# Two of five one-hot tiles per step move from VectorE to ScalarE in the last part of a graph kernel's scatter

## The reference

```python
q = (x_norm @ Wq + bq).reshape(num_nodes, NH, HD)
k = (x_norm @ Wk + bk).reshape(num_nodes, NH, HD)
v = (x_norm @ Wv + bv).reshape(num_nodes, NH, HD)
scores = jnp.einsum('ehd,ehd->eh', q[src], k[tgt]) / np.sqrt(HD).astype(np.float32)
scores = scores + (curv @ Wc + bc)
smax = jax.ops.segment_max(scores, tgt, num_segments=num_nodes)
p = jnp.exp(scores - smax[tgt])
probs = p / jax.ops.segment_sum(p, tgt, num_segments=num_nodes)[tgt]
messages = (probs[:, :, None] * v[tgt]).reshape(scores.shape[0], -1)
out = jnp.zeros_like(x).at[src].add(messages)
```

## Time and profile before

| | us |
|---|---|
| median of 3 runs | 8923.19 |
| lowest to highest | 8923.06 to 8924.19 |
| the profiled execution, its own time | 8924.33 |
| its span, first to last instruction | 8922.3 |

### The profile page before, as it was taken

One profiled execution on the slowest core, in us unless ns is written; L12 is line 12 of the kernel. 1 busy time (PEld: TensorE's weight loads), 2 busy tenths in 40 slices (PEclk: granted clock), 3 DMA queues, 4 the chain that ended last, 5 costly groups with the idle time before them and its releaser, 6 DMA issues. The chain is left out here.

```text
span 8922.3 us, 172430 instructions
## 1 busy us (share of the span) xinstructions
PE 6527.5 (73%) x29604; PEld 5175.7 (58%) x29605; DVE 5892.7 (66%) x18026; ACT 2572.9 (29%) x6876; POOL 6456.8 (72%) x6759
## 2 busy tenths in 40 slices
PE   6555555555788888888888988888745677666667
PEld 4433333333555555555688888888734566666555
DVE  4444444444566666666688888888854776766767
ACT  3111111111011111111355555555433333333322
POOL 6777777776777777777677777777757777777752
PEclk7566666666555555555555555555556777877778
DMA  5222222222222222222455555555435666666652
GB/s 199 61 65 67 66 65 66 66 65 64 54 63 62 62 63 62 62 63 62 102 137 136 136 136 136 136 136 136 121 81 126 154 154 152 156 154 154 154 139 77
DMA packets 1031683, 926.16 MB, mean 104 GB/s; under 512 B 210913, under 2 KB 911477, under 8 KB 1031495
## 3 DMA queue, kind: packets, MB, share of 16 engines
q0 software_dynamic: 214496, 443.25, 18.3%
q1 hardware_dynamic: 627671, 341.67, 15.1%
q10 hardware_dynamic: 189400, 139.98, 7.8%
HBM read 734.34 MB, written 192.49 MB: 104 GB/s over the span
## 5 line engine op out<-in xcount | busy, mean ns | idle before, releaser
L599 PE MATMUL stage_ps_agg<-stage_hot,stage_msg 128*128 128x128 f32 x6656 | 1587.4, 414 | 1221.6 <-DMA stage_msg<-xt,stage_index 890.7
L599 PEld LDWEIGHTS stage_ps_agg<-stage_hot,stage_msg 128*128 128x128 f32 x6656 | 1377.5, 306 | 1519.2 <-issue 662.4
L1174 POOL DMA_INDIRECT big<-q,stage_index x1664 | 1597.2, 960 | 547.3 <-issue 489.0
L1631 POOL DMA_INDIRECT slots<-big,stage_index x1664 | 1603.2, 963 | 510.6 <-issue 442.0
L588 POOL DMA_INDIRECT stage_msg<-xt_next,stage_index x1664 | 1570.7, 944 | 531.0 <-issue 520.3
L588 POOL DMA_INDIRECT stage_msg<-xt,stage_index x1664 | 1570.3, 944 | 530.3 <-issue 487.6
L631 DVE TENSOR_TENSOR big<-big,stage_ps_agg 128x128 f32 x3328 | 951.7, 286 | 1350.5 <-PE stage_ps_agg L599 989.8
L577 ACT ACTIVATE stage_index<-big 128x4 int32 (+1 forms) x832 | 170.3, 205 | 3607.3 <-PE stage_ps_agg L599 3509.1
L1668 PE MATMUL stage_ps_val<-nodes_a,big 128*128 x3328 | 672.4, 366 | 656.8 <-ACT big L1594 635.1
L1668 PEld LDWEIGHTS stage_ps_val<-nodes_a,big 128*128 128x128 f32 x3328 | 592.4, 267 | 719.0 <-issue 718.3
L1684 PE MATMUL stage_ps_sums<-stage_hot,big 128*128 128x128 f32 x4160 | 754.9, 345 | 112.0 <-DVE big L1804 107.1
(11 more groups left out here) (306 smaller groups left out, 9675.2 us busy)
## 6 DMA issues: line engine op xcount, KB each, us to landing
big<-slots SPq DMA_DIRECT2D x1976, 66.0 KB
big<-in_edge_attr_dram SPq DMA_DIRECT2D x1664, 64.0 KB
stage_trow<-targets ACTq DMA_DIRECT2D x830, 128.0 KB
stage_msg<-xt,stage_index POOLq DMA_INDIRECT x1664
stage_msg<-xt_next,stage_index POOLq DMA_INDIRECT x1664
big<-q,stage_index POOLq DMA_INDIRECT x1664
slots<-big,stage_index POOLq DMA_INDIRECT x1664
xt_next<-stage_xo SPq DMA_DIRECT2D x98, 256.0 KB, 2.9
```

The source lines that it names most:

```text
L599: last = self.nc.tensor.matmul(self.ps[h][:, j, :], self.msg[q][:, j, :], self.hot[h][:, j, :], start=True, stop=True)
L1174: pool.indirect_dma_start(qrow[q][:, j * D:(j + 1) * D], None, d["q"], bass.IndirectOffsetOnAxis(ap=index[q][:, j:j + 1], axis=0))\
L1631: pool.indirect_dma_start(d["slots"], bass.IndirectOffsetOnAxis(ap=index[q][:, j:j + 1], axis=0), total[q][:, j, :], None).then_inc(s_sc[q ...
```

## The change

In the last part VectorE's one-hot instruction covers three tiles (j = 2, 3, 4), 384 columns. ACT makes the other two (j = 0, 1): for each tile |place - n| into the new buffer `away` (two instructions of 128 columns, the place as a bias per partition), then relu(1 - away) for both tiles in one instruction of 256 columns into `hot`. For whole numbers this is 1 where n equals the place and 0 elsewhere.

ACT does it in the same queue in which it issues its two DMAs: a step waits for the freed buffer, issues the DMAs of step y, then makes the one-hot rows of step y-2. ACT's first four steps are written out, 12 turns of four steps follow in the loop, and the one-hot rows of the last two steps stand behind it. TensorE waits for one more semaphore (`s_act_hot`) in these steps. SP's part is the same as before, written in place of the shared function. The seven other parts don't change.

```diff
+    turns, SHARE, BY_SP, BY_ACT = GP // SLOTS, 3, 2, 2
+    away = slots("away", 2, [P, BY_ACT, P])
+    s_act_hot, s_away = m.sem("c_act_hot"), m.sem("c_away")
...
-        last_part(act, mybir.EngineType.Activation, SHARE, SET)
+        for q in range(SLOTS):
+            act.wait_ge(s_sc[q], TURNS * 16 * G + at[q])
+
+        def make_hot(y, h):
+            ring_index(act, s_place, y + 1, passed)
+            for j in range(BY_ACT):
+                nc.scalar.activation(away[h][:, j, :], t["iota"][:, :], ACT.Abs, scale=-1.0, bias=place[h][:, j:j + 1])\
+                    .then_inc(s_away, 1)
+            ring_index(act, s_away, (y - (PARTS - 1) * GP) * BY_ACT + BY_ACT, passed)
+            nc.scalar.activation(hot[h][:, 0:BY_ACT, :], away[h][:, :, :], ACT.Relu, bias=1.0, scale=-1.0)\
+                .then_inc(s_act_hot, 1)
+
+        def step(i, q):
+            y = i * SLOTS + (q + (PARTS - 1) * GP)
+            act.wait_ge(s_sum, y + 1)
+            r = offsets(nc, mybir.EngineType.Activation, pair_row, y * STRIDE + SHARE, SET - SHARE, (K - 1) * P)
+            for j in range(SHARE, SET):
+                act.dma_start(rows[q][:, j, :], d["slots"][bass.ds(r[j - SHARE], P), :]).then_inc(s_rows[q], 16)
+            if not isinstance(i, int) or y >= (PARTS - 1) * GP + 2:
+                make_hot(y - 2, q % 2)
+
+        for q in range(SLOTS):
+            step(0, q)
+        act.addr_align(256, max_nops=1)
+        with act.Fori(1, turns) as i:
+            for q in range(SLOTS):
+                step(i, q)
+        for y in range(SETS - 2, SETS):
+            make_hot(y, y % 2)
...
                 pe.wait_ge(s_hot, x.at() + (1 - FIRST))
+                if not x.within(0, FIRST, GROUPS + LAG):
+                    pe.wait_ge(s_act_hot, x.at() + (1 - LAG - GROUPS))
...
+                by_act = 0 if x.within(1, FIRST, GROUPS + LAG) else BY_ACT
...
-                nc.vector.tensor_tensor(hot[h][:, :, :], ps_lane[:, 0:P].unsqueeze(1).to_broadcast([P, SET, P]),
-                                        place[h][:, :].unsqueeze(2).to_broadcast([P, SET, P]), ALU.is_equal)\
+                nc.vector.tensor_tensor(hot[h][:, by_act:SET, :],
+                                        ps_lane[:, 0:P].unsqueeze(1).to_broadcast([P, SET - by_act, P]),
+                                        place[h][:, by_act:SET].unsqueeze(2).to_broadcast([P, SET - by_act, P]),
+                                        ALU.is_equal)\
                     .then_inc(s_hot, 1)
```

More of the change, by code:

```diff
@@ L1528, in scatter @@
     marks = (0, FIRST, GROUPS, LAST)
-    turns, SHARE, BY_SP = GP // SLOTS, 3, 2
+    turns, SHARE, BY_SP, BY_ACT = GP // SLOTS, 3, 2, 2
+    away = slots("away", 2, [P, BY_ACT, P])
+    s_act_hot, s_away = m.sem("c_act_hot"), m.sem("c_away")
     block = m.stack.enter_context(nc.Block())
[L1532 to L1543, removed]
     def load_targets(engine, g, q):
@@ L1575, in _ @@
                         sp.dma_start(rows[q][:, j, :], d["slots"][bass.ds(r[j], P), :]).then_inc(s_rows[q], 16)
-        last_part(sp, mybir.EngineType.SP, 0, SHARE)
+        for q in range(SLOTS):
+            sp.wait_ge(s_sc[q], TURNS * 16 * G + at[q])
+        sp.addr_align(256, max_nops=1)
+        with sp.Fori(0, turns) as i:
+            for q in range(SLOTS):
+                y = i * SLOTS + (q + (PARTS - 1) * GP)
+                sp.wait_ge(s_sum, y + 1)
+                r = offsets(nc, mybir.EngineType.SP, pair_row, y * STRIDE, SHARE, (K - 1) * P)
+                for j in range(SHARE):
+                    sp.dma_start(rows[q][:, j, :], d["slots"][bass.ds(r[j], P), :]).then_inc(s_rows[q], 16)
     @block.scalar
```

## The result

| | before | after |
|---|---|---|
| median of 22 runs each, us | 8924.40 | 8937.99 |
| lowest to highest | 8920.56 to 8927.70 | 8935.70 to 8943.86 |
| span of the profiled execution | 8922.3 | 8934.1 |

The change makes the kernel slower by 13.6 us: the ratio is 1.0016, with a 95% interval of 1.0010 to 1.0022. The forecast was 8935, 12 us more than before, in a range of 8922 to 8944.

A forecast was written before the change was run, and what follows sets the result against it. The prediction took SP's DMA-issuing queue to bound the last part, with ACT's queue taking over: 9.8 us from ACT's queue plus 2 from the ring, 12 us on 8924.3, less 1.1 for the median, gives 8935, range 8922 to 8944.

The forecast's parts named there:

- SP's queue bounds the last part: Last part before the change: SP's queue, issuing three row DMAs a step, runs without pause at 2.51 us per step.
- VectorE's step: VectorE's own step in the last part before: 0.20 to the one-hot, 0.96 to the first add, 1.15 adds, sum 2.31 us.
- One of its signs: VectorE idle before `place`, first instruction of its step: 24.8 of 29.9 us for row DMAs, read as rows issued too slowly.
- The one-hot: VectorE's last-part comparison, 640 to 384 columns: 825 to 553 ns, 14 us less busy time, gain on the path 0.
- the window load between one-hot and adds: VectorE's queue loads five windows into registers, 0.59 us, so in the loop adds start 0.96 us after the one-hot's start.
- the 12 steps outside the loop: VectorE's last-part steps outside its loop: only these could win something from the shorter one-hot; no size given.
- ACT's queue: ACT's last-part queue becomes the bound at 2.74 us per step against SP's 2.51: 9.8 us over 42 steps; chance 0.60.
- The ring: Sum frees ACT, ACT issues and makes one-hot, PE sums: at half clock 0.1 us per step over the queue, 2 us.
- a rival: PE's clock mostly at half in the last part, ring 2.95 us per step: 20 us, 8943; chance 0.18, dearer queue included.
- SP's waits: SP's last-part queue should wait for sums over 8 us in all, where it waited 0.3 before.
- VectorE's busy time: Should fall by 14 us through the shorter one-hot, while ACT's busy time rises by about 55 us.
- The tail: After ACT's last step: two more one-hots, about 1.1 us each, beside last rows and VectorE's adds; cost 0.

The follow-up runs named there:

- e2: Kernel before with only VectorE's one-hot cut to three tiles, nobody making the other two: 42 steps of the last part 104.1 us, before 104.0.
- e1: Kernel before, but in the last part SP issues two of a step's five row DMAs and ACT three: 42 steps 103.9 us, before 104.0.
- e9: Kernel before with last-part row DMAs issued by SP two, ACT two, GpSimd one, VectorE making all one-hots: 42 steps 101.5 us, before 104.0.
- e10: The change with row DMAs issued by SP two, ACT one, GpSimd two: 42 steps 102.0 us, the change 117.8, before 104.0.
- e3: Kernel before plus ACT's one-hot work with constant bias into unread buffers, VectorE making five tiles, PE not waiting for ACT: 42 steps 113.8 us, before 104.0.
- e6: The change with ACT's one-hot work put ahead of its buffer wait and DMA issues in each step: 42 steps 114.9 us, the change 117.8.
- e12: The kernel of e9 with the last part written out on all five queues instead of loops: 42 steps 90.6 us, ratio to before 0.9981.

## Why the prediction was right, point by point

*SP's queue bounds the last part: shown, with a second bound close behind.* e2 shows that VectorE's instruction is not the bound, e1 that a queue with three issues sets the same pace on ACT as on SP, and e9 that relieving the queues helps. But e9 gained 2.5 us and not more, since VectorE's queue was next, at 2.36 us per step before and 2.45 with e9's extra wait. The prediction put VectorE's step at 2.31 and left out the branch of VectorE's loop, although it charged SP's. This had no effect on the forecast. One of its signs was weaker than it read: of the 24.8 us that `place` waited for rows, 17.0 are the first wait of the part, and the 42 steps hold only 5.0.

```profile
DVE stage_place L1785 <- DMA big<-slots: 24.8, 14, 17.0
```

SP's rows without a pause carry the argument, not this sum.

*The one-hot: 553 ns and no gain.* Measured 558, and e2 and e10 show the zero. The reason given for it, the window load between one-hot and adds, is what the trace shows (0.92 from one to the other, now with 0.36 idle). It hoped for something in the 12 steps outside the loop; they gave nothing either, 0.82 to 0.83 before and after.

*ACT's queue: 2.74 per step.* e3 and e6 run at 2.74. The terms: two Abs 0.69 (said 0.68), Abs end to Relu start 0.12 (said 0.13), an undisturbed step 2.65 (said 2.67 without the branch), a step with the branch 2.95 to 3.0 (said 0.3 more). The Relu is 0.42, not 0.38, and beside the next register load, as said. For the Abs pair the Trainium skill (ScalarE: Activation LUTs, What ACT_TABLE_LOAD costs) gave an estimate of 0.681, and the trace agrees with 0.69. The queue's share of the loss was forecast as 9.8 us; e3 has 9.8.

*The ring: this term was too small, and for two reasons.* The prediction gave it 2 us, from 0.1 per step in four of ten steps. It is 3 to 4. The time of one passage was right: two steps of the change behind a sum at half clock take 2.99 + 2.65 = 5.64 us (8701.96 to 8707.60), where it said 5.6 to 5.7. But it set this against two mean steps, 2 x 2.74, and the mean has the branch in it. Where one of the two steps has the branch, the queue alone takes 2.65 + 2.95, and the ring all but hides behind it. Where neither has, the queue takes 2 x 2.65 = 5.30, and a passage costs 0.34. Of ACT's 42 steps eight without the branch are 2.98 to 3.13 long; what they have above 2.65 is 2.9 us. The other reason is that sums at half clock became more frequent. The mean clock of the last part fell from 0.83 to 0.70, and PE's sums show it:

```profile
8695.95 2.50 PE L1712 MATMUL stage_ps_sums<-stage_hot,big 128*128 128x128 f32 x10 [1.27 <-ACT stage_hot L1623]
8698.64 2.50 PE L1712 MATMUL stage_ps_sums<-stage_hot,big 128*128 128x128 f32 x10 [0.19 <-ACT stage_hot L1623]
8701.67 2.50 PE L1712 MATMUL stage_ps_sums<-stage_hot,big 128*128 128x128 f32 x10 [0.54 <-ACT stage_hot L1623]
```

It took the clock for given at its level before the change, and kept the fall for a rival. The rival was partly right: nearly six in ten steps at half clock ((2.02 - 1.38) / (2.50 - 1.38) from the mean length of the 52 sums), where the forecast had four and the same reckoning gives three for the kernel before (mean 1.73). The hand-overs were as short as hoped (0.13 us from the Relu's end to the matmuls), so the ring cost 3 to 4 us and not the 10 that this rival had on top of the queue's share. With its own 0.1 per step, six in ten would have made only 2.4 us. That the forecast of 12 us came within 2 of the 13.6 is thus the queue's term, and the error on the ring was small because the ring is.

*The rest.* SP's waits were to be over 8 us, and are 13.1. VectorE's busy time was to fall by 14 us, and fell by 13.4 over the kernel (5892.7 to 5879.3); ACT's was to rise by 55, and rose by 57.4 (2572.9 to 2630.3). `place` stands 2.81 us apart, the sum's 2.74 and the ring. The tail was to cost nothing, and the steps outside the 42 add 0.4.

*Open.* What exactly makes PE's clock fall in the change wasn't tried by itself. The kernels here with clearly longer steps have the lower clock. In e6 it is 0.74 and the pace is still the queue's, so there the lower clock cost nothing that shows.

## What to carry to other kernels

Before work is moved to an engine that looks idle, add up its queue: register loads, DMA issues, waits and the branch don't count as busy time, and ACT, at 0 us busy in this stage, had only 0.7 us of room in a step of 2.5 while the work needed 0.97. And ask what stands behind the instruction that gets shorter: here VectorE's own register load and SP's queue, so the cut was worth nothing even when it was free. Where every queue of a stage is nearly full of small instructions, look for an idle queue and for straight code in the last few dozen steps: together they brought 16 us here, and none of the shifts of arithmetic that were tried brought anything.

## What I had not expected of the hardware

- The register load of row numbers depends on how many it loads: 0.283 us for one and 0.494 for two on ACT, 0.707 for three; on SP 0.475 for two and 0.667 for three. Yet VectorE loads five in 0.590. So moving an issue moves its share of the load too. The row for one, from e10:

```profile
L1078 ACTq TENSOR_LOAD <-spare x49: 279/283/296, 8659.8 to 8780.6; - x49
```

- GpSimd's direct DMA issues were cheap enough: two in a step with their register load (0.51 us) kept up with 2.43 us per step (e10).
- Written-out code of 52 steps on five queues was cheaper than the loops; steps in e12 are 2.08 and 2.09 us over long stretches. Nine of the 42 steps are 2.16 to 2.71, about 3 us more in all; whether the fetching of code is among the causes was not looked into.
- PE's mean granted clock goes with the pace: 0.94 at 2.16 us per step (e12), 0.83 at 2.48 (before), 0.70 at 2.81 (the change). Which of the two drives the other wasn't separated. The Trainium skill (TensorE: Matmul & The Clock Gate, Part 1) says that activity releases the throttle; within this stage the traces agree.
